# Order of work inside a tile: a third maximum product and the splits for coming groups behind the gated rows

## The reference, cut to what matters

```python
xn = _layernorm(x, axis=-1)
x = x + attn(xn, ...) + ffn(xn, ...)
# ffn: top 2 of 16 experts for each row, with weights that sum to 1
xs = flat[sorted_tok]
g = jax.lax.ragged_dot(xs, gate_w, group_sizes)
u = jax.lax.ragged_dot(xs, up_w, group_sizes)
h = jax.nn.silu(g) * u
dn = jax.lax.ragged_dot(h, down_w, group_sizes)
routed = jnp.zeros_like(flat).at[sorted_tok].add(sorted_w[:, None] * dn)
# attn: causal, q and k of 64 numbers each
scores = jnp.einsum('btd,bsd->bts', q, k) * scale
attn = jax.nn.softmax(jnp.where(causal[None], scores, -1e30), axis=-1)
```

## Time and profile before

| | before |
|---|---|
| median of 3 runs | 1816.95 us (1816.46 to 1821.04) |
| the profiled execution | 1810.25 us, of which span 1808.4 us |
| PE busy | 1729.9 us (96%) |
| PE weight loads busy | 1379.7 us (76%) |
| DVE busy | 1169.6 us (65%) |
| ACT busy | 751.4 us (42%) |
| POOL busy | 664.0 us (37%) |
| `routed`, from the first `egu` load | 696.99 us to about 1482 us of the span |

### The profile page before, as it was taken

How to read it: one execution, slowest core, us unless ns; L and a number is a source line. 1 busy time by engine, 2 the same in 40 slices (tenths; PEclk the granted TensorE clock), 3 DMA queues, 4 the chain that set the end, 5 groups by cost and what they waited for, 6 DMA issues and landing times. The chain is left out here.

```text
span 1808.4 us, 27930 instructions
## 1 busy us (share of the span) xinstructions
PE 1729.9 (96%) x8349; PEld 1379.7 (76%) x8349; DVE 1169.6 (65%) x2284; ACT 751.4 (42%) x1296; POOL 664.0 (37%) x676
## 2 busy tenths in 40 slices
PE   5699999999999998999999999999999989999998
PEld 3588787787777786788778877778888867777776
DVE  7777677777777663455555555555555537878787
ACT  3232332233223322333333333333333348878885
POOL 2544554445454442333433433433433421111110
PEclk9799999999999999999999999999999999999999
DMA  7767777756777655644544546555444429799896
GB/s 251 247 197 229 244 224 216 254 194 194 209 230 228 209 180 189 206 136 155 181 174 165 175 164 200 181 179 178 159 167 168 175 52 186 196 250 217 213 254 168
DMA packets 149933, 352.50 MB, mean 195 GB/s; under 512 B 20476, under 2 KB 41916, under 8 KB 149824
## 3 DMA queue, kind: packets, MB, share of 16 engines
q1 hardware_dynamic: 97276, 234.52, 39.1%
q0 software_dynamic: 43968, 104.91, 22.6%
q10 hardware_dynamic: 8580, 11.64, 2.3%
HBM read 208.24 MB, written 146.70 MB: 196 GB/s over the span
## 5 line engine op out<-in xcount | busy, mean ns | idle before, releaser
L1488 POOL DMA_INDIRECT expert_rows<-res,ids_all x143 | 149.8, 1048 | 446.3 <-ACT res L1309 437.3
L1429 DVE TENSOR_REDUCE mx<-emb 128x1 f32<-128x512 f32 (+3 forms) x288 | 175.0, 641 | 107.3 <-PE emb L1228 85.9
L70 PE MATMUL egu<-w,rT_0h 128*128 x576 | 186.4, 405 | 0.8 <-DVE rT_0l L1400 0.8
L70 PE MATMUL egu<-w,rT_1h 128*128 x568 | 182.7, 403 | 0.0
L1406 DVE TENSOR_TENSOR eh<-egu,esg 128x256 f32<-128x256 f32 x143 | 60.6, 424 | 182.9 <-ACT esg L1299 182.9
L1035 POOL DMA_INDIRECT token_list<-tok,slot x128 | 126.6, 989 | 116.6 <-DVE slot L741 80.7
L1686 ACT ACTIVATE ex<-sc 128x1024 f32<-128x1024 f32 (+4 forms) x176 | 144.3, 821 | 60.1 <-PE sc L1631 42.7
L1483 POOL DMA_INDIRECT rows<-xn_scratch,rows_all x137 | 132.6, 968 | 48.7 <-issue 43.1
L1299 ACT ACTIVATE esg<-egu 128x256 f32<-128x256 f32 x143 | 55.0, 384 | 202.9 <-PE egu L70 200.2
L1758 POOL DMA_DIRECT2D base<-expert_rows x32 | 41.8, 1538 | 252.2 <-DMA base<-base_scratch 231.4
L1630 PE MATMUL sc<-qh,khl 128*128 128x512 f32 (+3 forms) x288 | 113.1, 393 | 14.4 <-ACT pr_1h L1686 4.5
(11 more groups left out here) (283 smaller groups left out, 4506.1 us busy)
## 6 DMA issues: line engine op xcount, KB each, us to landing
w<-expert_parts SPq DMA_DIRECT2D x64, 768.0 KB, 7.8
base<-expert_rows POOLq DMA_DIRECT2D x32, 1024.0 KB, 12.8
expert_parts<-ew_h SPq DMA_DIRECT2D x32, 768.0 KB, 7.3
expert_parts<-ew_l SPq DMA_DIRECT2D x32, 768.0 KB, 8.5
x<-x SPq DMA_DIRECT2D x16, 1024.0 KB, 6.2
xn_scratch<-xn SPq DMA_DIRECT2D x16, 1024.0 KB, 8.3
base_scratch<-xb SPq DMA_DIRECT2D x16, 1024.0 KB, 11.7
base<-base_scratch SPq DMA_DIRECT2D x16, 1024.0 KB, 11.3
```

What stands on the lines that cost most here:

```text
L70: mm = pe.matmul(dst, w, m, start=(first and i == 0), stop=(last and i == len(terms) - 1))
L1429: dve.tensor_reduce(mx[n % 2][:, j, c:c + 1], mb[g % 2][:, 0:width], AX.X, ALU.max).then_inc(m_red, 1)
L1488: pool.indirect_dma_start(parts_d[:, :], bass.IndirectOffsetOnAxis(ap=ids_all[:, t:t + 1], axis=0), res[t % 2][:, :], None, bounds_check=2 ...
```

## The change

Three moves, all inside a tile:

- on PE, the maximum products beyond the second come behind `turn_hidden(t)`, not ahead of it;
- on ACT, the splits for coming groups come behind `hidden_turned(t)`;
- on DVE, the reductions beyond the second and the splits for coming groups come behind `hidden_turned(t)`.

```diff
@@ PE
                     max_scores(g, t)
                 if t + 2 < TILES:
                     turn(t + 2)
-                for g in maxima(t)[2:]:
-                    max_scores(g, t)
                 if t == LAST_SLOT + 2:
                     turn_lowest()
                 if FOLD <= t < FOLD + 3:
                     fold_weights(t - FOLD)
                 turn_hidden(t)
+                for g in maxima(t)[2:]:
+                    max_scores(g, t)
@@ ACT
                 if t > 0:
                     downed(t - 1)
+                hidden_turned(t)
                 for n, which in splits[t]:
                     split_high(n, which)
-                hidden_turned(t)
```

## The result

| | before | changed |
|---|---|---|
| median, 8 runs each | 1817.03 us (1814.09 to 1824.13) | 1811.17 us (1808.69 to 1813.25) |
| ratio | | 0.996 (0.9947 to 0.9973) |
| profiled execution | 1810.25 us, span 1808.4 | 1808.9 us, span 1807.1 |
| tile 3 to tile 141 of the routed stage | 754.87 us | 745.72 us |
| PE busy | 1729.9 us | 1730.2 us |

The change is faster, by 5.9 us; 18.7 us were forecast, with a range that ended at 1808. It went the forecast way with less than a third of the size.

A forecast was written before the change was run, and what follows sets the result against it. PE was taken to bound the routed stage. Third maximum 10.0 us plus splits 8.7 us made 18.7 us, off the 1816.95 us median: 1798.2 us forecast, range 1791 to 1808 us.

The forecast's parts named there:

- PE is the bound, moves only take away waits: Routed stage: PE busy 698.35 of 707 us; the moves shorten no PE instruction, only its waits.
- Third maximum, 10.0 us: PE, tiles with three maxima: 28 save 0.38 us each of 0.48 lost, less 0.6 us for two load-block tiles.
- lower bound of 0.22 us: PE, least saving per three-maxima tile: the undisturbed length of the two gated-row transposes.
- The third reduction: DVE: wanted by the next tile's first maximum product 4.2 us in, ends by 2.7; no cost.
- Splits, 8.7 us: ACT and DVE: late down products recover 7.0 us behind 13 split tiles and 1.7 us in four load-block tiles.
- `load_block` stands behind the next `esg`: ACT queue: `load_block` comes after the next `esg`, so work queued behind the moved splits costs nothing.
- Margins of `eh` and `esg`: DVE and ACT: idle time of 1.49 and 1.53 us plus 1.1 us margin of `eh` absorbs the moved work.
- rivals 3 to 5: Another PE feeder, 1816.95 us (0.06); ACT delays `esg`, 1825.9 (0.04); POOL holds DVE subtractions, 1813.3 (0.04).
- Load blocks stay, about 7 us: ACT, ten load blocks without a split: about 7 of 18.4 us of down-product waits remain.
- Sum: Whole kernel: 10.0 + 8.7 = 18.7 us gain, all on PE.
- Rival 2: PE: third product's wait only half used, 0.22 us saved per three-maxima tile, 14.3 us gain, 1802.7 us; chance 0.16.

The follow-up runs named there:

- between: Changed kernel with the extra product between gate_up and down, its reduction ahead of `eh` on DVE; ratio 0.9884 to before, stage 735.68 us.
- head_first: Changed kernel with the next tile's head on PE (register instruction and waits) ahead of the third product; ratio 0.9925 to before, stage 741.80 us.
- third_only: Kernel before with only the third product and its reduction moved behind the gated rows, splits left in place; ratio 0.9996, stage 754.36 us.
- splits_only: Kernel before with only the splits moved behind `hidden_turned` on ACT and DVE, third product left in place; ratio 0.9947, stage 748.23 us.
- head_late_wait: head_first with the wait for the reductions (`m_red`) moved behind the down products; ratio 0.9935 to before, stage 741.26 us.
- loads_apart: Changed kernel with `load_block` behind `hidden_turned`, three DMA issues there, two a tile later (groups 2, 10 unchanged); ratio 0.9912 to before, stage 739.01 us.
- third_late_wait: third_only with the wait for the reductions (`m_red`) moved behind the down products; ratio 0.998 to before, stage 749.55 us.

## Why the prediction was wrong, point by point

- **PE is the bound, moves only take away waits:** right. PE's busy sum rose by 0.3 us and the clock stayed.
- **Third maximum, 10.0 us: the step that failed.** "After the third load the next `egu` load can follow at once", so 0.38 of 0.48 us for each tile. The wait, the place of the transposes and the time of the third load all came as forecast; the saving was 0.13 us. The 0.40 us between the first `ehb` load and the next `egu` load was taken for the transposes' cost. Most of it was time that stands behind a blocked product in any case (about 0.2 us more than behind a free one, by between), over which the transposes had lain, and the tile head's instructions (0.11 to 0.14 us, by head_first), which they had covered too. With 28 x 0.13 = 3.6 us this alone is 6.4 us under the term, and under the lower bound of 0.22 us: the transposes had cost less than their ordinary length, since part of them was hidden. This bound rested on their length in a tile without a block.
- **The third reduction: wrong.** "Wanted by the next tile's first maximum product 4.2 us in." Its wait stands in `maxima_ready`, ahead of the down products, 2.6 us in. It costs nothing where all is in time, 0.65 us in tile 23, and 3 us behind split tiles in third_only; in the changed kernel the splits' move took that off, and tiles 6, 23 and 70 stay.
- **Splits, 8.7 us: right in the main part.** 7.0 us behind 13 tiles went, as forecast. The 1.7 us of tiles with a load block did not come, for three reasons. In tiles 6 and 70 the split gave its part back (0.84 to 0.48 and 0.22 to nothing in splits_only), and the third reduction took it again (1.08 and 0.28 in the changed kernel; 0.30 and nothing in head_late_wait, where its wait stands behind the down products). In tile 72 the issues on ACT are counted from the tile's own start, so a wait that goes ahead of them comes back behind them; the prediction says this of tiles 23 and 70 and not of 72. Tile 7 varies with the length of its issues. "`load_block` stands behind the next `esg`", at no cost, was wrong there: its wait for the moved v subtraction delays the issues by 0.53 us.
- **Margins of `eh` and `esg`:** right; rivals 3 to 5 are out. The DVE subtraction at 922.83 ran beside the scatter that POOL began at 922.82 and took 0.71 us, not 0.69. All 16 k subtractions lie over a scatter or gather of POOL in both kernels, at 0.69 us on average before and 0.71 changed, and no `eh` was late for them. The Trainium skill ("SBUF — State Buffer", section "Who interferes with whom") says that DVE work with two inputs in SBUF contends with GpSimd's reads; no block for a whole instruction shows here.
- **Load blocks stay, about 7 us:** right, and loads_apart took 6.7 us off all load tiles.
- **Sum:** 18.7 forecast, 9.15 in the stage. Third maximum 6.4 too much; the load tiles 1.7 too much, and another 0.4 lost there (8.3 to 8.7), of which tile 56 alone is 0.43 (last section); tiles with two maxima 0.9 (5.216 to 5.225 us, 99 of them). These make 9.4 of the 9.55 us. The medians gave 5.9 and 8.6 us, less than the stage in both comparisons; that its later start took the rest fits the profiles and is not shown. Rival 2, a half-used wait, named the right weakness, but was priced at 0.22 us for a tile.

## What to carry to other kernels

A wait in front of a product on PE cost more here than the wait: the blocked product itself showed for about 0.2 us more than a free one, and each register instruction after it for 0.15 us, where a tile without a block hid them. Put the blocked instruction where its wait is over, and not where other work merely covers a part of it; what stood behind it had been free. Before a gain is summed, look for waits that stand at the head of a block for something used at its end, and for work on another engine that is timed from the start of the same tile: a wait removed ahead of that comes back. Follow every semaphore that a moved instruction raises, also into an engine that looks idle.

## What the runs showed of the hardware

A register instruction on PE costs nothing in a tile where no product is blocked (5.23 us with one and with three) and 0.15 us each right behind a blocked product. One DMA issue of a load block holds ACT's queue for 0.6 us as a rule, 0.33 us at the least, and some of them for up to 1.45 us (L1318 of the kernel before) or 1.59 us (splits_only), not in the same tiles each time. The start of a weight load can run ahead of the pace of the products: in head_first the first `egu` load came early, and the down product's load followed 2.79 us behind it, not 2.64. In both profiles of the changed kernel and in six others, `esg` of tile 56 started 0.4 to 0.5 us late (3.49 us into the tile in the changed kernel, not 3.06) with no cause in the profile, while its `egu` products had run on time; both profiles of the kernel before, splits_only, third_late_wait and between do not show it. That stays open.
